# Reordering one step of a perceiver block kernel: row sums ahead of the second row maxima, PV ahead of the last quarter of a projection, tile 2's quantisation behind tile 0's third layer norm

## The chip, the cores and the metric

The kernel runs on one core of a Trainium2 chip. The metric is the time of one execution on the device in microseconds (us); the number given is the median of several executions. TensorE (PE) has a full clock of 2.4 GHz and a lower level of 1.2 GHz; the profile states the granted clock as a share of the full one.

## The reference

The input `x` is 16 x 64 rows of 1024 floats, the context 16 matrices of 1024 x 1024 floats (67 MB). Three residual blocks follow one another:

```python
# 1: cross attention stand-in: both sides fake-quantised to 8 bits
q1 = fake_quant(layernorm(x));  q2 = fake_quant(ctx_4096)
x = x + matmul(q1, q2)                       # per batch element
# 2: multi-query attention, 32 heads of 32, ALiBi, causal
qkv = layernorm(x) @ Wqkv
probs = softmax(where(causal, q @ k.T * scale + alibi, -1e30))
x = x + (probs @ v).reshape(B, S, H) @ Wo
# 3: routed one-bit feed-forward layer
h = layernorm(x);  r = softmax(h @ gate_w.T)
x = x + (h * (r @ in_scale)) @ sign(weight).T * (r @ out_scale) + bias
```

## The kernel before

The 1024 rows are cut into eight tiles of 128 rows (two batch elements, `b` = 0 and 1). Each tile needs 8 MB of context, which arrives as eight pieces of 1 MB in a ring of four slots: `load_context` on SyncE (SP) issues piece `c` of tile `t` to slot `c % 4`, after the piece that lay there has been rounded to 8 bits. That rounding is `conv(t, c)`, line 583 on ScalarE (ACT), now and then line 955 on VectorE (DVE). Two pieces make one call `context(t, pair)`, 8 matmuls at line 1407, and four calls are the product of block 1. I write "piece 2.4" for piece 4 of tile 2.

The quantised rows of a tile are made on DVE: `norm0_rows` (lines 979 and 983), then `norm0_quant` (lines 986 and 988), which writes `a16` and raises the semaphore `s_a`. From tile 2 on the rows are transposed by a DMA, `turn_over`, that SP issues when `s_a` has come. For tile 2 this call stands in SP's queue between the loads of pieces 2.0 to 2.3 (and the bias) and those of 2.4 to 2.7, so these four loads are issued only after it.

Every engine has its order of work written out by hand. The sequence is an entry, `step_0`, `step_1`, and then for tiles 2 to 7 an `opening` and a `burst` (tile 2 has no opening of its own). `step_1(s, ahead)` covers the heads of tile 1, the second half of tile 0's attention (`s`), all of tile 1's attention after the scores (`ahead`), both output projections, tile 0's feed-forward layer and the context product of tile 2. The names of its parts:

- `scores(s, h)` on PE, and on DVE `scores_in(t, h, b)` (line 1058) and `row_max(t, h, b)` (line 1063); `softmax_in(t, h)` is both for `b` = 0 and 1. `subtract_max` (line 334) runs on GpSimd (POOL) in this step, `exp` (line 605) on ACT, `row_sum` (lines 1068 and 1069) on DVE, `normalize` (line 485) on POOL. `pt` transposes the probabilities on PE (line 1426), `pt_hi` (line 567, ACT) and `pt_lo` (line 892, DVE) split them into two halves of 16 bits. `pv(s, h)` is the product with V (line 1507), `o_hi` (line 635, ACT) and `o_lo` (line 1081, DVE) split its result.
- `project(s, n, ks)`: half `n` of the output projection, three matmuls of 512 columns for each of the `ks` (lines 1371 to 1373); `low` is `k` = 0 to 3, `high` is 4 to 7. `x2(s, n)` on DVE adds it to `X` (line 1093) and takes half of the row statistics (line 959); after the second half POOL makes the inverse deviation, `inv_std(2, .)` (lines 458 and 459), and DVE `norm2` (line 971). `x1` (line 1007) and its statistics, `inv_std(1, .)` and `norm1` (line 971) are the same for block 1, and `t1` transposes what `norm1` wrote; `t1_hi` and `t1_lo` split that, and `kv(2)` begins the next tile.
- `t2` transposes what `norm2` wrote, `t2_copy` (line 567, ACT) takes it to `ln2T`, `router` (line 1554, PE), `router_max`, `router_exp` (line 697, ACT), `router_probs` (lines 1126 to 1132, DVE), `router_t` (line 1561), `rt_copy` (ACT), `inscale` (line 1573), `xs` (line 1140), `xs_hi` (ACT), `xs_lo` (DVE), `outscale` (line 1589), `outscale_copy` (line 613), `ffn` (line 1603), `result` (line 1154).

Matmul results lie in eight banks: `C` (two), `R` (four), and `T` (two, used in turn, so that each user waits until the one before it but one has been emptied). POOL's order at the end of the step is `with_bias(0)`, `with_row_sum(2)`, `inv_std(0, 3)`, `inv_std(2, 1)`, `inv_std(1, 2)`.

Of the kernel before, what the change touches and what calls it, by code (L numbers as in the profile page):

```python
# [139 lines left out]
def build(nc, x, context, wqkv, wo, w_t, bias, quant_in, small_in, scales_in, out):  # L140
    ctx = ExitStack()
    with ctx:
# [188 lines left out]
        def subtract_max(e, t, h, b):  # L331

            e.wait_ge(s_mx, piece(t, h, b) + 1)
            e.tensor_tensor(by_head(h, b), by_head(h, b), to_heads(h, b), ALU.subtract)\  # L334
                .then_inc(s_sub[b], 1)
# [100 lines left out]
        @block.gpsimd  # L436
        def _(e):

            chain = Chain(e, s_pool)
            link = chain.link  # L440

            e.memset(rs[:, 3:4], 0.0).then_inc(s_warm, 1)
            e.memset(bfill[:, BRING * H // 2:], BASE_PAIR).then_inc(s_fill, 1)
            for m in (ident, ident_h):
                link(e.memset(m[:, :], 0.0))
                link(e.affine_select(out=m[:, :], in_=m[:, :], compare_op=ALU.not_equal,
                                     fill=1.0, base=0, pattern=[[-1, P]], channel_multiplier=1))
            for hi, lo in vbd:
                link(e.memset(hi[:, :, :], 0.0))
                link(e.memset(lo[:, :, :], 0.0))  # L450
            for k, value in enumerate((-0.5, EPS)):
                link(e.memset(consts[:, k:k + 1], value))
            e.nop().then_inc(s_init, 1)

            def inv_std(k, t):

                e.wait_ge(s_st[k], t + 1)
                link(e.tensor_tensor(rstd[k][:, 0:1], mv[k][:, 1:2], consts[:, 1:2], ALU.add))  # L458
                e.tensor_tensor(rstd[k][:, 1:2], rstd[k][:, 0:1], consts[:, 0:1], ALU.pow)\
                    .then_inc(s_rstd[k], 1)  # L460

            def with_row_sum(t):

                e.wait_ge(s_row, t + 1)
                x_t = X[t % XBUFS]
                e.tensor_tensor(x_t[:, :], x_t[:, :], rowsum[:, 1:2].broadcast_to([P, H]), ALU.add)\  # L466
                    .then_inc(s_xc, 1)

            def with_bias(m):
                if m == 0:  # L470
                    e.wait_ge(s_bias, 16)
                e.wait_ge(s_xl2, m + 1 + (m == TILES - 1))
                x_m = X[m % XBUFS]
                e.tensor_tensor(x_m[:, :], x_m[:, :], bias_sb[:, :], ALU.add).then_inc(s_x2b, 1)

            def total(t, n):
                cols, x_t = slice(n * HALF, (n + 1) * HALF), X[t % XBUFS]
                e.wait_ge(s_fe, t * 2 + n + 1)
                if n == 0:
                    e.wait_ge(s_x2b, t + 1)  # L480
                e.tensor_tensor(x_t[:, cols], x_t[:, cols], XL[:, cols], ALU.add).then_inc(s_y, 1)  # L481

            def normalize(t, h, b):
                e.wait_ge(s_rcp, piece(t, h, b) + 1)
                e.tensor_tensor(by_head(h, b), by_head(h, b), to_heads(h, b), ALU.mult).then_inc(s_nrm, 1)  # L485

            def entry():
                inv_std(0, 0)
                with_row_sum(0)
                inv_std(0, 1)  # L490
                with_row_sum(1)

            def step_0(s):
                inv_std(1, 0)
                subtract_max(e, 0, 0, 0)
                subtract_max(e, 0, 0, 1)

            def step_1(s, ahead):
                subtract_max(e, 0, 1, 0)
                subtract_max(e, 0, 1, 1)  # L500
                normalize(0, 0, 0)
                normalize(0, 0, 1)
                inv_std(1, 1)
                normalize(0, 1, 0)
                normalize(0, 1, 1)
                inv_std(0, 2)
                subtract_max(e, 1, 0, 0)
                subtract_max(e, 1, 0, 1)
                subtract_max(e, 1, 1, 0)
                subtract_max(e, 1, 1, 1)  # L510
                normalize(1, 0, 0)
                normalize(1, 0, 1)
                normalize(1, 1, 0)
                normalize(1, 1, 1)
                inv_std(2, 0)
                with_bias(0)
                with_row_sum(2)
                inv_std(0, 3)
                inv_std(2, 1)
                inv_std(1, 2)  # L520
                total(0, 0)
                total(0, 1)

            def opening(s):
                m = s.i - 1
                subtract_max(e, m, 1, 1)
                normalize(m, 1, 0)
                normalize(m, 1, 1)
                with_bias(s.i - 2)
                total(s.i - 2, 0)  # L530
                inv_std(1, s.i)
                if s.next:
                    inv_std(0, s.i + 1)
                total(s.i - 2, 1)

            def burst(s):
                if not s.is_step(2):
                    inv_std(2, s.i - 1)
                if s.next:
                    with_row_sum(s.i + 1)  # L540
                subtract_max(e, s.i, 0, 1)
                normalize(s.i, 0, 0)
                normalize(s.i, 0, 1)

            def tail(s, last):
                t = TILES - 1
                subtract_max(e, t, 1, 1)
                normalize(t, 1, 0)
                normalize(t, 1, 1)
                with_bias(t - 1)  # L550
                total(t - 1, 0)
                inv_std(2, t)
                with_bias(t)
                total(t - 1, 1)
                x_t = X[t % XBUFS]
                for n in range(2):
                    cols = last_cols[n]
                    e.wait_ge(s_fe, t * 2 + n + 1)
                    e.tensor_tensor(x_t[:, cols], x_t[:, cols], XL[:, cols], ALU.add).then_inc(s_y, 1)

            run_steps(entry, step_0, step_1, opening, burst, tail)


        @block.scalar
        def _(e):
# [37 lines left out]
            def exp(t, h, b):  # L603
                e.wait_ge(s_sub[b], t * 2 + h + 1)
                e.activation(heads(h, b), heads(h, b), ACT.Exp).then_inc(s_exp, 1)  # L605
# [142 lines left out]
            def step_1(s, ahead):  # L748
# [27 lines left out]
                exp(1, 0, 1)  # L776
                sign(3)
                exp(1, 1, 0)
                exp(1, 1, 1)
                pt_hi(ahead, 0, 0)  # L780
                pt_hi(ahead, 0, 1)
                conv(2, 0)
                o_hi(ahead, 0)
                pt_hi(ahead, 1, 0)
# [2 lines left out]
                conv(2, 2)  # L787
                o_hi(ahead, 1)
                conv(2, 3)
                conv(2, 4)  # L790
                t2_copy(s, 0)
                t2_copy(s, 1)
                router_exp(s)
                conv(2, 5)
                rt_copy(s)
# [89 lines left out]
        def _(e):  # L885
# [325 lines left out]
            def step_1(s, ahead):  # L1211
# [23 lines left out]
                softmax_in(1, 0)  # L1235
                o_lo(s, 1)
                q_lo(s, 1)
                softmax_in(1, 1)
                row_sum(1, 0, 0)
                row_sum(1, 0, 1)  # L1240
                norm0_rows(2)
                row_sum(1, 1, 0)
                row_sum(1, 1, 1)
                pt_lo(ahead, 0, 0)
                pt_lo(ahead, 0, 1)
                norm0_quant(2)
                o_lo(ahead, 0)
                x2(s, 0)
                x2(s, 1)
                pt_lo(ahead, 1, 0)  # L1250
                pt_lo(ahead, 1, 1)
                norm2(s)
                o_lo(ahead, 1)
                stats0(3)
                router_max(s)
# [3 lines left out]
                xs(s, 1)  # L1259
                xs_lo(s, 0)  # L1260
                xs_lo(s, 1)
                x2(ahead, 1)
                x1(ahead)
                norm1(ahead)
                result(ahead, 0)
                t1_lo(ahead, 0)
# [82 lines left out]
        def _(e):  # L1349
# [5 lines left out]
            low, high = range(KT // 2), range(KT // 2, KT)  # L1355
# [304 lines left out]
            def step_1(s, ahead):  # L1660
# [13 lines left out]
                tk(s)  # L1674
                query(s, 0, high[:2])
                pt(s, 1, 0)
                pt(s, 1, 1)
                query(s, 0, high[2:])
                query(s, 1, low)
                pv(s, 1)  # L1680
                scores(s, 0)
                query(s, 1, high)
                project(s, 0, low)
                scores(s, 1)
                project(s, 1, low)
                project(s, 0, high)
                pt(ahead, 0, 0)
                pt(ahead, 0, 1)
                project(s, 1, high)
                pv(ahead, 0)  # L1690
                pt(ahead, 1, 0)
                pt(ahead, 1, 1)
                project(ahead, 0, low)
                pv(ahead, 1)
                project(ahead, 1, low)
                t2(s)
                context(2, 0)
                router(s)
                project(ahead, 0, high)
                router_t(s)  # L1700
                context(2, 1)
                inscale(s, 0)
                inscale(s, 1)
                project(ahead, 1, high)
                context(2, 2)
                context(2, 3)
                ffn(ahead, 0, low)
                outscale(ahead, 0)
                outscale(ahead, 1)
                ffn(ahead, 0, high)  # L1710
                ffn(ahead, 1, low)
                t1(ahead)
                ffn(ahead, 1, high)
# [125 lines left out]
```

## Time and profile before

| | before |
|---|---|
| median of 3 runs | 408.12 us (407.4 to 408.24) |
| profiled execution, own time | 407.38 us |
| its span | 405.6 us |
| PE matmul busy | 362.7 us, 89% of the span |
| DVE / ACT / POOL busy | 312.1 / 253.8 / 133.5 us |
| transfers | 91.56 MB, 226 GB/s over the span |

The span is divided into busy time of each engine; an engine's work is strictly in the order of its own queue, and between engines semaphores decide. `step_1` runs from about 55 us to 134 us, where `kv(2)` begins. The tables below name for each instruction its start, its duration and, in brackets, how long its engine had been idle and what ended that.

### The profile page before, as it was taken

To read this page: it belongs to the slowest core of one execution; us is meant where nothing else is said; L and a number is where in the kernel's file an instruction comes from. 1 tells how busy PE (TensorE), PEld (TensorE's weight loads), DVE (VectorE), ACT (ScalarE), POOL (GpSimd) and SP (SyncE) were. 2 spreads that over 40 slices of the span, in tenths; PEclk is the share of its full clock that TensorE was granted. 3 is DMA by queue.
4 is the path that set the end of the run, shared out by engine and by line. 5 is a ranking of instruction groups with operands and counts; after the bars stand their busy time and mean duration, and the time that the engine had idled before them with its cause. 6 is when DMAs were issued, how large, how long until landed. Compare 5 with 4: busy or idle time off the path is not lost.

```text
span 405.6 us, 10034 instructions
## 1 busy us (share of the span) xinstructions
PE 362.7 (89%) x4162; PEld 233.9 (58%) x4162; DVE 312.1 (77%) x592; ACT 253.8 (63%) x306; POOL 133.5 (33%) x148
## 2 busy tenths in 40 slices
PE   0438977999789999999999999999999999999996
PEld 0113943874444874578557855696559655974444
DVE  6888798999846788679876997589858975496353
ACT  3857985867787877783887388648865741334021
POOL 5320043426321226312541246124612371026041
PEclk9957999999999999999999999999999999999999
DMA  7999999399999499857867587748665000100002
GB/s 303 410 373 408 409 405 391 114 322 412 311 367 347 190 288 404 302 178 196 298 229 240 147 269 263 228 153 294 225 244 131 10 2 6 50 2 0 2 1 105
DMA packets 30243, 91.56 MB, mean 226 GB/s; under 512 B 8112, under 2 KB 8496, under 8 KB 30192
## 3 DMA queue, kind: packets, MB, share of 16 engines
q1 hardware_dynamic: 28320, 84.42, 58.5%
q10 hardware_dynamic: 1872, 6.40, 4.2%
q8 instruction: 39, 0.64, 0.6%
q14 instruction: 12, 0.10, 0.1%
HBM read 85.05 MB, written 4.19 MB: 220 GB/s over the span
## 4 chain that ended last, share of the span: by engine, by line
PE 60%; DVE 15%; DMA 9%; ACT 7%; SPq 4%; issue 3%; POOL 0%; DVEq 0%; ACTq 0%; POOLq 0%
DMA ring<-ctx 9%; PE R L1603 9%; PE T L1426 6%; PE R L1371 5%; PE R L1372 5%; PE R L1373 5%; PE C L1407 4%; ACT b L583 4%; PE R L1462 4%; PE R L1465 3%; PE R L1464 3%; PE T L1507 3%; SPq L371 2%; PE R L1491 2%; PE R L1378 1%
## 5 line engine op out<-in xcount | busy, mean ns | idle before, releaser
L583 ACT ACTIVATE b<-ring,quant,qpar 128x2048 uint8<-128x2048 f32 x61 | 126.4, 2093 | 14.3 <-DMA ring<-ctx 8.2
L1462 PE MATMUL R<-T_hi,Wqkv_hi 128*128 128x128 f16 x448 | 77.9, 220 | 0.0
L1465 PE MATMUL R<-T_hi,Wqkv_lo 128*128 128x128 f16 x448 | 77.7, 219 | 0.0
L1464 PE MATMUL R<-T_lo,Wqkv_hi 128*128 128x128 f16 x448 | 77.7, 219 | 0.0
L1407 PE MATMUL C<-b,aT 128*64 128x512 f16 x256 | 35.7, 411 | 12.9 <-ACT b L583 6.3
L485 POOL TENSOR_TENSOR Pr<-Pr,mx 128x512 f32<-128x512 f32 x32 | 35.4, 1118 | 30.5 <-DVE mx L1069 30.5
L334 POOL TENSOR_TENSOR Pr<-Pr,mx 128x512 f32<-128x512 f32 x20 | 20.7, 1044 | 74.7 <-DVE mx L1063 74.7
L1462 PEld LDWEIGHTS R<-T_hi,Wqkv_hi 128*128 128x128 f16 x448 | 43.9, 98 | 2.0
L1464 PEld LDWEIGHTS R<-T_lo,Wqkv_hi 128*128 128x128 f16 x448 | 43.9, 98 | 0.2
L1465 PEld LDWEIGHTS R<-T_hi,Wqkv_lo 128*128 128x128 f16 x448 | 43.8, 98 | 0.0
L1371 PE MATMUL R<-Wo,attT_hi 128*128 128x512 f16 x112 | 42.5, 379 | 0.6 <-DVE attT_lo L1081 0.5
L1372 PE MATMUL R<-Wo,attT_hi 128*128 128x512 f16 x112 | 42.4, 379 | 0.0
L1373 PE MATMUL R<-Wo,attT_lo 128*128 128x512 f16 x112 | 42.4, 379 | 0.0
L1603 PE MATMUL R<-sgn,XS_hi 128*128 128x512 fp8e4 x96 | 36.6, 381 | 0.0
L1603 PE MATMUL R<-sgn,XS_lo 128*128 128x512 fp8e4 x96 | 36.4, 379 | 0.0
L959 DVE BATCH_NORM_STATS2 st<-X 128x6 f32<-128x512 f32 x48 | 33.1, 689 | 1.4
L481 POOL TENSOR_TENSOR X<-X,XL 128x512 f32<-128x512 f32 x14 | 17.8, 1271 | 41.0 <-DVE XL L1154 40.1
L458 POOL TENSOR_TENSOR small<-small,consts 128x1 f32<-128x1 f32 x24 | 4.6, 192 | 77.1 <-DVE small L966 77.1
L1407 PEld LDWEIGHTS C<-b,aT 128*64 128x64 f16 x256 | 13.5, 115 | 27.1 <-ACT b L583 8.3
L466 POOL TENSOR_TENSOR X<-X,small 128x1024 f32<-128x1024 f32 x8 | 16.6, 2075 | 34.2 <-DVE small L991 34.2
L567 ACT ACTIVATE PT_hi<-T 128x512 f16<-128x512 f32 x32 | 17.6, 593 | 15.9 <-PE T L1426 15.8
L605 ACT ACTIVATE Pr<-Pr 128x512 f32<-128x512 f32 x32 | 19.8, 625 | 11.3 <-DVE Pr L334 10.5
(172 smaller groups left out, 845.4 us busy)
## 6 DMA issues: line engine op xcount, KB each, us to landing
ring<-ctx SPq DMA_DIRECT2D x64, 1024.0 KB, 7.7
ring<-L_attn_Wo SPq DMA_DIRECT2D x4, 1024.0 KB, 9.3
ring<-L_ffn_weight SPq DMA_DIRECT2D x4, 1024.0 KB, 5.2
Wo<-L_attn_Wqkv SPq DMA_DIRECT2D x7, 544.0 KB, 15.2
X<-x ACTq DMA_DIRECT2D x6, 512.0 KB, 4.6
out<-X ACTq DMA_DIRECT2D x6, 512.0 KB, 6.2
X<-x SPq DMA_DIRECT2D x2, 512.0 KB, 11.5
sgn<-L_attn_Wqkv SPq DMA_DIRECT2D x1, 544.0 KB, 18.0
```

The lines of the kernel that those rows point to most:

```text
L485: e.tensor_tensor(by_head(h, b), by_head(h, b), to_heads(h, b), ALU.mult).then_inc(s_nrm, 1)
L583: e.activation(b8[:, c % BRING, :], ring[:, slot, :], ACT.Identity, scale=qR2, bias=qZ2).then_inc(s_rf[slot], 1)
L959: link(e.bn_stats(st[k][:, h, :], src[:, h * HALF:(h + 1) * HALF]))
L1371: e.matmul(dst, lhs[0], rhs[0], start=first, stop=False)
L1372: e.matmul(dst, lhs[0], rhs[1], start=False, stop=False)
L1373: return e.matmul(dst, lhs[1], rhs[0], start=False, stop=last)
L1407: ins = e.matmul(C[b * S:(b + 1) * S, n, :], lhs(b), b16[:, (2 * pair + b) % BRING, k, n * HALF:(n + 1) * HALF], start=first, stop=last)
L1426: last = e.transpose(T[:, bank, n * P:(n + 1) * P], src, ident[:, :])
L1462: e.matmul(dst, hi, rows[0], start=k == 0 and g == 0, stop=False, skip_group_check=True)
L1464: e.matmul(dst, hi, rows[1], start=False, stop=False, skip_group_check=True)
L1465: last = e.matmul(dst, lo, rows[0], start=False, stop=k == KT - 1, skip_group_check=True)
L1603: last = e.matmul(ffn_to(s.i - 2, n), XS[part][:, k, :], sgn[:, k, n * HALF:(n + 1) * HALF], start=k == 0 and part == 0, stop=k == KT - 1 ...
```

## The change

Orders alone change, in `step_1`; no instruction is added or removed. POOL: the normalisation of the first half of tile 1's heads goes ahead of the subtraction of the maxima of the second half. ACT: `exp(1, 1, 1)` goes behind the two `pt_hi` of the first half; `conv(2, 4)` goes behind the two `t2_copy`. DVE: the row sums of the first half go ahead of the row maxima of the second half, the last row sum goes behind two `pt_lo`, `norm0_quant(2)` goes from ahead of `o_lo(ahead, 0)` to behind `norm2(s)`, and `x1(ahead)` goes ahead of `x2(ahead, 1)`. PE: as listed. SP's queue is left as it is.

```diff
 POOL    inv_std(0, 2)
         subtract_max(e, 1, 0, 0)
         subtract_max(e, 1, 0, 1)
+        normalize(1, 0, 0)
+        normalize(1, 0, 1)
         subtract_max(e, 1, 1, 0)
         subtract_max(e, 1, 1, 1)
-        normalize(1, 0, 0)
-        normalize(1, 0, 1)
 ACT     exp(1, 1, 0)
-        exp(1, 1, 1)
         pt_hi(ahead, 0, 0)
         pt_hi(ahead, 0, 1)
+        exp(1, 1, 1)
         conv(2, 0)
...
-        conv(2, 4)
         t2_copy(s, 0)
         t2_copy(s, 1)
+        conv(2, 4)
         router_exp(s)
 DVE     q_lo(s, 1)
-        softmax_in(1, 1)
+        scores_in(1, 1, 0)
+        scores_in(1, 1, 1)
         row_sum(1, 0, 0)
         row_sum(1, 0, 1)
+        row_max(1, 1, 0)
+        row_max(1, 1, 1)
         norm0_rows(2)
         row_sum(1, 1, 0)
-        row_sum(1, 1, 1)
         pt_lo(ahead, 0, 0)
         pt_lo(ahead, 0, 1)
-        norm0_quant(2)
+        row_sum(1, 1, 1)
         o_lo(ahead, 0)
         x2(s, 0)
         x2(s, 1)
         pt_lo(ahead, 1, 0)
         pt_lo(ahead, 1, 1)
         norm2(s)
+        norm0_quant(2)
         o_lo(ahead, 1)
...
         xs_lo(s, 1)
+        x1(ahead)
         x2(ahead, 1)
-        x1(ahead)
         norm1(ahead)
 PE      pt(s, 1, 0)
+        query(s, 0, high[2:3])
         pt(s, 1, 1)
-        query(s, 0, high[2:])
+        query(s, 0, high[3:])
         query(s, 1, low)
         pv(s, 1)
+        query(s, 1, high[:1])
         scores(s, 0)
-        query(s, 1, high)
+        query(s, 1, high[1:])
...
-        project(s, 1, high)
+        project(s, 1, high[:3])
         pv(ahead, 0)
+        project(s, 1, high[3:])
         pt(ahead, 1, 0)
         pt(ahead, 1, 1)
         project(ahead, 0, low)
         pv(ahead, 1)
         project(ahead, 1, low)
         t2(s)
+        project(ahead, 0, high)
+        router(s)
         context(2, 0)
-        router(s)
-        project(ahead, 0, high)
+        context(2, 1)
         router_t(s)
-        context(2, 1)
         inscale(s, 0)
         inscale(s, 1)
         project(ahead, 1, high)
         context(2, 2)
         context(2, 3)
         ffn(ahead, 0, low)
+        ffn(ahead, 0, high)
         outscale(ahead, 0)
         outscale(ahead, 1)
-        ffn(ahead, 0, high)
         ffn(ahead, 1, low)
         t1(ahead)
```

## Rows read from the trace of the kernel before

**Rows 1.** Busy time by stretch, with count; last columns: granted clock, DMA share, GB/s
```profile
84.00:111.60 27.60, 24.10 (x208) 13.64 (x209) 24.90 (x43) 19.92 (x19) 11.52 (x11) 1.00 0.98 359
111.60:134.00 22.40, 20.68 (x188) 9.84 (x187) 13.10 (x27) 18.36 (x17) 5.48 (x9) 1.00 0.97 355
134.00:180.00 46.00, 45.23 (x571) 30.97 (x568) 35.60 (x74) 35.13 (x47) 16.46 (x17) 1.00 0.80 276
180.00:222.00 42.00, 41.93 (x511) 28.11 (x508) 34.17 (x69) 29.09 (x37) 15.19 (x16) 1.00 0.71 233
```

**Rows 2.** Timeline of PE: start, duration, instruction, idle time before it
```profile
104.39 0.63 PE L1426 MATMUL T<-ident,Pr 128*128 128x128 f32 x4 [1.69 <-DVE attT_lo L1081]
114.70 0.81 PE L1554 MATMUL T<-ln2T,small_sb 128*8 128x32 f32 x64 [1.04 <-ACT ln2T L567]
122.53 1.92 PE L1407 MATMUL C<-b,aT 128*64 128x512 f16 x16
131.06 1.09 PE L1426 MATMUL T<-ident,tok 128*128 128x128 f32 x8 [0.69 <-DVE tok L971]
```

**Rows 3.** Timeline of DVE from tile 1's split probabilities to tile 0's norm 2
```profile
100.25 1.24 DVE L892 TENSOR_TENSOR PT_lo<-T,PT_hi 128x512 f16<-128x512 f32 x2
101.41 0.55 DVE L986 TENSOR_SCALAR a<-a 128x1024 int16<-128x1024 int16 x1
101.98 1.28 DVE L988 TENSOR_SCALAR_CACHE_REDUCE a<-a,qpar 128x1024 f16<-128x1024 int16 x1
103.50 0.75 DVE L1081 SCALAR_TENSOR_TENSOR attT_lo<-T,attT_hi 128x256 f16<-128x256 f32 x2
108.45 0.81 DVE L971 TENSOR_SCALAR XL<-X,small 128x1024 f32<-128x1024 f32 x1
```

**Rows 4.** Timeline of SP's queue around the transposing transfer of tile 2
```profile
103.30 1.33 SPq L385 DMA_TRANSPOSE aT<-a  x1
104.69 0.57 SPq L371 DMA_DIRECT2D ring<-ctx  x1
```

**Rows 5.** Issues in 104.6 to 105 us: KB, us to landing (piece 2.4)
```profile
ring<-ctx SPq DMA_DIRECT2D x1, 1024.0 KB, 5.2
aT<-a SPq DMA_TRANSPOSE x1, 3.4
```

**Rows 6.** Busy time by stretch, columns as in group 1
```profile
116.00:120.00 4.00, 4.00 (x29) 1.80 (x27) 2.52 (x9) 3.88 (x4) 0.00 (x0) 1.00 1.04 416
```

**Rows 7.** Timeline of ACT from piece 2.3 to the feed-forward input
```profile
110.00 4.07 ACT L583 ACTIVATE b<-ring,quant,qpar 128x2048 uint8<-128x2048 f32 x2
113.98 1.06 ACT L567 ACTIVATE ln2T<-T 128x512 f32<-128x512 f32 x2
116.05 0.30 ACT L697 ACTIVATE rt<-rl,small 128x8 f32<-128x8 f32 x1 [1.01 <-DVE small L1120]
118.58 4.07 ACT L583 ACTIVATE b<-ring,quant,qpar 128x2048 uint8<-128x2048 f32 x2
122.55 1.13 ACT L567 ACTIVATE XS_hi<-ln2T 128x512 f16<-128x512 f32 x2
```

**Rows 8.** Timeline of DVE, from the split input to tile 2's norm 1
```profile
117.26 0.17 DVE L1132 TENSOR_TENSOR rstack<-rt,rstack 128x16 f16<-128x16 f32 x1
123.19 1.29 DVE L892 TENSOR_TENSOR XS_lo<-ln2T,XS_hi 128x512 f16<-128x512 f32 x2 [2.11 <-ACT XS_hi L567]
124.41 0.68 DVE L1093 SCALAR_TENSOR_TENSOR X<-R,X 128x512 f32<-128x512 f32 x1
126.09 1.27 DVE L1007 SCALAR_TENSOR_TENSOR X<-C,qpar,X 128x1024 f32<-128x1024 f32 x1
130.19 0.81 DVE L971 TENSOR_SCALAR tok<-X,small 128x1024 f32<-128x1024 f32 x1 [1.01 <-POOL small L459]
```

**Rows 9.** Timeline of POOL, the two inverse deviations at the step's end
```profile
126.25 0.19 POOL L458 TENSOR_TENSOR small<-small,consts 128x1 f32<-128x1 f32 x1 [11.85 <-DVE small L966]
129.26 0.19 POOL L458 TENSOR_TENSOR small<-small,consts 128x1 f32<-128x1 f32 x1 [2.18 <-DVE small L966]
```

**Rows 10.** The longest idle time of PE at full clock: timeline, then the stretch
```profile
24.45 1.92 PE L1407 MATMUL C<-b,aT 128*64 128x512 f16 x8 [5.06 <-ACT b L583]
...
22.00:24.00 2.00, 0.00 (x0) 0.00 (x0) 1.86 (x5) 1.69 (x1) 0.16 (x1) 0.57 0.97 307
```

## The prediction

> **What bounds the kernel now.** I read the busy time by stretch first. From 180 us on PE is busy 41.93 of 42.00 us, and in 134 to 180 us 45.23 of 46.00 [rows 1]: from tile 2 on the kernel is a full PE queue, and what `step_1` gains or loses arrives at the end nearly whole. At most 0.8 us could be made good in tile 2's burst, where PE still waits a little. From 84 to 134 us PE is busy 24.10 and 20.68 of 50.0 us [rows 1], so 5.2 us idle: that is the most this change can win. In the same stretches the transfers are at a share of 0.98 and 0.97 [rows 1], which no later stretch shows. The reader should see both: PE has holes here, and the DMA has none to spare.
>
> Then the timelines. PE's holes of interest are 1.69 us ahead of `pt(ahead, 1, 1)`, which waits for `o_lo(ahead, 0)`; 1.04 us ahead of `router`, which waits for `ln2T`; and the one ahead of `t1(ahead)` at 131.06 us, which waits for `norm1` [rows 2]. Between them `context(2, 2)` and `context(2, 3)` run without a gap, 122.53 to 124.45 [rows 2]. Yet they are just in time: ACT rounds 2.6 and 2.7 in one row 118.58 to 122.65 [rows 7], and the second call starts at about 123.4, only 0.8 us later. Last, SP's queue: the transposing transfer goes out at 103.30, the moment `norm0_quant(2)` ends (101.98 + 1.28 = 103.26), and the load of 2.4 at 104.69, right behind it [rows 3, 4].
>
> **Part 1, the front of the step (all moves up to `pv(ahead, 1)`): a gain on PE.** Row sums ahead of row maxima: on DVE two maxima of 0.6 us come out of the way, so the first `normalize` starts some 1.2 us sooner and the hole between the two first `pt` closes. The three quarters of `project` go under `pt_hi` and `pt_lo`, the query slices fill two short waits; the waits they fill end on DVE, so they save 0.4 us at the second `scores`. The large piece is `norm0_quant(2)` out of the way of `o_lo`: 0.55 + 1.28 + 0.28 us, about 2.1 [rows 3]. The price on this side is that `exp(1, 1, .)` comes about 2 us later, because POOL normalises first; `row_sum(1, 1, 1)` then stands behind `pt_lo` and costs it nothing. Followed instruction by instruction: `pt_lo` ends at 100.4 (1.0 sooner than 101.41, [rows 3]), `row_sum(1, 1, 1)` to 101.2, `o_lo` 101.5 to 102.2, and `pt(ahead, 1, 1)` starts at 102.35 where it was 104.39 [rows 2]. PE is **2.0 us ahead** here, and stays so through `project(ahead, 1, low)`.
>
> **Part 2, router behind the projection: another 1.0 us, on paper.** `t2_copy` no longer waits for `conv(2, 4)` (2.04 us of the pair 110.00 to 114.07, [rows 7]) and `project(ahead, 0, high)`, 12 matmuls, covers it: the hole of 1.04 [rows 2] goes. Up to there PE is about 3 us ahead of before.
>
> **Part 3, `norm0_quant(2)` behind `norm2(s)`: what SP makes of it.** Between the old place of `norm0_quant` and its new one stand `o_lo`, two `x2`, two `pt_lo` and `norm2`, which took DVE from 103.50 to 109.26 without a hole, 5.8 us [rows 3]. The new start is `row_sum(1, 1, 1)`'s end 101.2, 0.3 for `o_hi`, and 5.8: 107.3. It takes 1.9 (101.41 to 103.26), so `s_a` comes at **109.3 instead of 103.3, 6.0 us later**. Nothing on DVE suffers, and `aT` itself is not missed: 109.3 plus 3.4 to 4.7 us for the transfer [rows 4, 5] is 112.7 to 114.0, and `context(2, 0)` now comes at 114.2, behind `router`. But SP is a queue, and behind `turn_over(2)` stand the loads of 2.4 to 2.7. Piece 2.4 went out at 104.69 and landed 5.2 us later, 109.9 [rows 4, 5]. Now it goes out 1.4 us after `s_a`, at 110.7, and lands at **115.9**. The DMA, at 0.98 before, stands nearly empty from the landing of the bias (about 106) to 111.
>
> The other three slots are free by then (conv of 2.1 to 2.3 ends by 110.3), so 2.5 to 2.7 go out at once behind 2.4 and follow at the full rate. 1.05 MB at 416 GB/s [rows 6] is 2.53 us each: 2.7 lands at 115.9 + 7.6 = 123.5. Before, its rounding began at about 120.6, half way in the pair of [rows 7]. So `conv(2, 7)` starts **3.0 us later** and ends at 125.6. The bounds: if the loads were to land at once after 2.4, ACT alone would need 115.9 + 3 x 2.04 + 0.6 (`router_exp`, `rt_copy`) = 122.6, still 2.0 later than before; if they came at 355 GB/s, the mean of these stretches [rows 1], 2.7 lands at 124.8, 4.2 later. I take 3.0, since a full queue is what the row with 416 shows.
>
> Two more things hang on this. `router_exp` now stands behind `conv(2, 4)` on ACT, which ends at 117.95, so it comes 1.9 us later than 116.05 [rows 7], and `router_t`, 1.2 us behind it (117.43 + 0.7 there [rows 7, 8]), at 119.4. PE has finished `context(2, 1)` at about 116.2 and idles 3.2 us, then again until `rt_copy`, which stands behind `conv(2, 5)`, 120.8. All that PE gained is given back here; it reaches `context(2, 2)` at 124.0 and waits for 2.7 until 125.6.
>
> Behind `conv(2, 7)` ACT makes `xs_hi`, then DVE `xs_lo`: from 122.65 to 124.41 before [rows 7, 8], 1.8 us. New: 127.4, which is 3.0 later. `context(2, 3)` is done by then (126.6).
>
> **Part 4, `x1(ahead)` ahead of `x2(ahead, 1)`: the queue of POOL.** `t1(ahead)` needs `norm1`, that needs `inv_std(1, 2)`, and on POOL `inv_std(2, 1)` still stands in front of it and needs the statistics of `x2(ahead, 1)`. Before, from 124.41 to `t1` at 131.06: `x2(ahead, 1)` 1.68, `x1` with statistics and hop 3.17 (126.09 to 129.26), `inv_std` 0.93 to 130.19, `norm1` 0.87, in sum 6.65 [rows 2, 8, 9]; `inv_std(2, 1)` ran at 126.25 beside the work [rows 9]. Now: `x1` 3.10, `x2(ahead, 1)` 1.84 with the hop to POOL, `inv_std(2, 1)` 0.87, then `inv_std(1, 2)` 0.93, `norm1` 0.87: 7.6. So **0.95 us more** than with the old order. The move could only pay where `x1` can start before `x2(ahead, 1)` could, and both are ready when `xs_lo` ends. `outscale` waits for `x2(ahead, 1)`'s first instruction at about 131.3 and `ffn(ahead, 1, low)` ends at 133.5, still ahead of `t1`, so moving it behind `ffn(ahead, 0, high)` hides that. The sum is thus bounded: 0.95 if both are ready, 0 if `x1` could start 1 us sooner than now, which `xs_lo` excludes.
>
> **The sum.** `t1` at 127.4 + 7.6 = 135.0 instead of 131.06: 3.0 + 0.95 = **4.0 us later**, and `kv(2)`, 2.7 us behind it in both, at 137.8 instead of 133.8. The profiled execution, 407.38 us (span 405.6), becomes 411.4. It lay 0.7 us under the median of the runs, so the median becomes **412.1**.
>
> **The rivals.** *The clock falls.* PE would be idle 3.2 us and, but for one transpose, 4.6 us, 116.2 to 120.8. The one idle time that long at full clock in this trace, 5.06 us before 24.45, had the granted clock at 0.57 of full in 22 to 24 us, so it went to the 1.2 GHz level under 3 us after PE stopped [rows 10]. Against it: mine is shorter and has work in it. If it falls, `inscale` and `project(ahead, 1, high)` (3.1 us) take 6.2 and end at 127 instead of 124, both context calls follow, and `x1` starts at 128.7 instead of 127.4: 1.3 us more, **413.4**. The Trainium skill (TensorE: Matmul & The Clock Gate, HAM oscillation) warns that PE-idle gaps between bursts drop the array to its slow level; by that rule this rival would be the likelier one, and the row agrees for a gap of 5.06 us, while none here shows 3.2.
>
> *The loads catch up.* ACT's own queue is the bound, 2.0 instead of 3.0, and tile 2's burst gives 0.4 back: **410.7**.
>
> *Faster.* If pieces 2.4 to 2.7 were not what is late, PE's lead decides: about 3 us up to `router`, less 0.95 for part 4, so 2.1 gained: **406.0**. It decides once 2.7 is rounded by the time PE reaches `context(2, 3)`, about 120.5; for that `s_a` would have to come by about 104.5. Only a `norm0_quant` that DVE reaches 5 us sooner than the rows add up to would do it. For it speaks that a DMA wait is often hidden; against it that this one has 0.8 us of cover.
>
> *Nothing in sum.* Lead and loss cancel to within 0.8 us: **408.1**. That needs 2.7 to land at about 120.
>
> **How the numbers follow.** Forecast 412.1 with a chance of 0.50; the clock 0.25; catching up 0.12; faster 0.08; nothing 0.05. The range takes in the first three and their bounds: below, 2.0 + 0.95 less 0.8 is 410.3; above, 4.2 + 0.95 is 413.3, and 413.4 with the clock, with another 0.8 for a clock that falls sooner: 414.2. About 0.2% (0.8 us) is what a measurement of this kernel can tell from no change. Faster 0.08, same 0.05, slower 0.87.
>
> **What would show it.** Right: the transposing transfer issued near 109.3; DMA nearly idle 106 to 111; piece 2.4 rounded from about 116; a PE hole ahead of `router_t` of about 3 us; `pt(ahead, 1, 1)` near 102.4; two `inv_std` back to back before `norm1`; `kv(2)` near 137.8. Wrong: the transfer before 107, or ACT rounding 2.4 to 2.7 with no wait for the ring, or `x1` starting well ahead of the end of `xs_lo`. A fallen clock around 120 us would show the first rival.

## The result and the profile after

| | before | changed |
|---|---|---|
| median of 4 runs each | 407.90 us (407.4 to 408.24) | 413.84 us (413.54 to 414.49) |
| profiled execution, own time | 407.38 us | 413.63 us |
| its span | 405.6 us | 411.8 us |
| PE matmul busy | 362.7 us | 366.3 us |
| DVE / ACT / POOL busy | 312.1 / 253.8 / 133.5 us | 311.2 / 253.6 / 134.7 us |

The ratio is 1.0147, with a 95% interval of 1.0132 to 1.0162: the changed kernel is **5.9 us slower**. The forecast was 412.1 in a range of 410.3 to 414.2.

Where the time went is seen in the same order as before. First SP's queue, the transposing transfer and what follows it (start, duration), then its landings (KB, us from issue), which answer to [rows 4, 5]:

```profile
96.11 0.47 SPq L414 DMA_DIRECT2D bias_sb<-L_ffn_bias  x1
109.51 1.34 SPq L385 DMA_TRANSPOSE aT<-a  x1
110.89 26.55 SPq L371 DMA_DIRECT2D ring<-ctx  x10
```

```profile
ring<-ctx SPq DMA_DIRECT2D x1, 1024.0 KB, 5.4
aT<-a SPq DMA_TRANSPOSE x1, 3.1
```

The transfer goes out at 109.51 instead of 103.30, and with it the load of 2.4 at 110.89 instead of 104.69. From about 106 us, when the bias has landed, the DMA stands still. This is the busy time by stretch (columns as in [rows 1]):

```profile
84.00:111.60 27.60, 25.38 (x217) 14.52 (x214) 24.93 (x44) 20.71 (x21) 13.44 (x12) 1.00 0.77 292
...
104.00:106.00 2.00, 2.00 (x11) 0.78 (x8) 1.79 (x5) 2.00 (x2) 0.00 (x0) 1.00 0.21 78
106.00:108.00 2.00, 1.52 (x15) 0.74 (x15) 2.00 (x4) 2.00 (x2) 0.77 (x3) 1.00 0.00 0
108.00:110.00 2.00, 2.00 (x11) 0.88 (x10) 1.93 (x5) 2.00 (x3) 2.00 (x1) 1.00 0.00 0
```

PE did win in front: it is busy 25.38 us up to 111.6, where it was 24.10 [rows 1]. But the DMA share fell from 0.98 to 0.77. ACT then waits for the ring at every one of the four pieces (in brackets: idle time, and what ended it), where [rows 7] show no such wait:

```profile
116.29 2.10 ACT L583 ACTIVATE b<-ring,quant,qpar 128x2048 uint8<-128x2048 f32 x1 [4.36 <-DMA ring<-ctx]
118.29 0.28 ACT L697 ACTIVATE rt<-rl,small 128x8 f32<-128x8 f32 x1
119.36 2.10 ACT L583 ACTIVATE b<-ring,quant,qpar 128x2048 uint8<-128x2048 f32 x1 [0.79 <-DMA ring<-ctx]
121.37 0.25 ACT L567 ACTIVATE rT<-T 32x128 f16<-32x128 f16 x1
122.88 2.10 ACT L583 ACTIVATE b<-ring,quant,qpar 128x2048 uint8<-128x2048 f32 x1 [1.27 <-DMA ring<-ctx]
125.44 2.10 ACT L583 ACTIVATE b<-ring,quant,qpar 128x2048 uint8<-128x2048 f32 x1 [0.46 <-DMA ring<-ctx]
```

The timeline of PE shows what is made of that, and answers to [rows 2]: one hole is smaller (0.94 for 1.69), the one ahead of `router` is gone, and two new ones stand ahead of `router_t` and `inscale`:

```profile
102.96 0.63 PE L1429 MATMUL T<-ident,Pr 128*128 128x128 f32 x4 [0.94 <-DVE attT_lo L1081]
...
119.79 0.22 PE L1564 MATMUL T<-ident_h,rstack 128*32 128x128 f16 x1 [3.41 <-DVE rstack L1132]
121.72 1.01 PE L1576 MATMUL T<-rT,scales 32*128 32x128 f16 x8 [1.71 <-ACT rT L567]
...
137.24 1.09 PE L1429 MATMUL T<-ident,tok 128*128 128x128 f32 x8 [1.40 <-DVE tok L971]
```

In the second of these holes the granted clock falls to its 1.2 GHz level, at about 121.1 us, and stays there for about 6.8 us (`inscale` takes 1.01 us where the same eight take 0.60 at full clock, in e1 below). Busy time by stretch:

```profile
118.00:120.00 2.00, 0.21 (x1) 0.09 (x1) 1.26 (x6) 1.21 (x3) 0.00 (x0) 1.00 1.03 410
120.00:122.00 2.00, 0.29 (x5) 0.32 (x5) 0.94 (x2) 1.61 (x2) 0.00 (x0) 0.77 1.01 406
122.00:124.00 2.00, 2.00 (x11) 0.97 (x10) 1.29 (x2) 1.12 (x1) 0.00 (x0) 0.50 1.04 414
124.00:126.00 2.00, 2.00 (x6) 0.65 (x5) 0.00 (x0) 1.54 (x2) 0.00 (x0) 0.50 1.02 406
126.00:128.00 2.00, 2.00 (x7) 0.56 (x7) 0.00 (x0) 2.00 (x3) 0.00 (x0) 0.52 1.03 414
```

Last, DVE from `x1` to `norm1`, and POOL's two inverse deviations, which answer to [rows 8, 9]. `x1` waits 0.47 us for `context(2, 3)`, which is late because the projection ahead of it ran at the lower clock; then both inverse deviations run one behind the other, after `x2(ahead, 1)`:

```profile
129.85 1.28 DVE L1007 SCALAR_TENSOR_TENSOR X<-C,qpar,X 128x1024 f32<-128x1024 f32 x1 [0.47 <-PE C L1410]
...
136.37 0.81 DVE L971 TENSOR_SCALAR tok<-X,small 128x1024 f32<-128x1024 f32 x1 [1.79 <-POOL small L459]
```

```profile
134.66 0.19 POOL L458 TENSOR_TENSOR small<-small,consts 128x1 f32<-128x1 f32 x1 [21.63 <-DVE small L966]
134.92 0.55 POOL L459 TENSOR_TENSOR small<-small,consts 128x1 f32<-128x1 f32 x1
135.44 0.19 POOL L458 TENSOR_TENSOR small<-small,consts 128x1 f32<-128x1 f32 x1
135.71 0.55 POOL L459 TENSOR_TENSOR small<-small,consts 128x1 f32<-128x1 f32 x1
```

`t1` is 137.24 - 131.06 = 6.2 us late, and so is the end: the span grew by 6.2. After tile 2's `kv` nothing is won or lost: in 186 to 228 us PE is busy 41.93 of 42.00 us, as in [rows 1].

### The profile page after: what moved, and what is told of

The parts are those of the page before. It is cut to its first block, busy times and chain, and to the rows that moved or that the text cites. A ratio compares the mean times of both kernels' runs of the same rounds, so it can differ in the third digit from the quotient of the medians.

```text
span 411.8 us, 10034 instructions
## 1 busy us (share of the span) xinstructions
PE 366.3 (89%) x4162; PEld 236.1 (57%) x4162; DVE 311.2 (76%) x592; ACT 253.6 (62%) x306; POOL 134.7 (33%) x148
## 4 chain that ended last, share of the span: by engine, by line
PE 63%; DVE 18%; DMA 7%; ACT 5%; issue 4%; POOL 2%; SPq 1%; DVEq 0%; POOLq 0%; ACTq 0%
PE R L1606 9%; DMA ring<-ctx 7%; PE T L1429 6%; PE R L1374 6%; PE R L1375 5%; PE R L1376 5%; PE C L1410 5%; PE R L1465 5%; PE R L1468 4%; PE R L1467 4%; PE T L1510 3%; PE R L1494 2%; DVE st L959 2%; ACT b L583 2%; PE R L1381 2%
## 5 line engine op out<-in xcount | busy, mean ns | idle before, releaser
L485 POOL TENSOR_TENSOR Pr<-Pr,mx 128x512 f32<-128x512 f32 x32 | 36.0, 1133 | 31.1 <-DVE mx L1069 31.1
L334 POOL TENSOR_TENSOR Pr<-Pr,mx 128x512 f32<-128x512 f32 x20 | 21.6, 1088 | 72.0 <-DVE mx L1063 72.0
L1374 PE MATMUL R<-Wo,attT_hi 128*128 128x512 f16 x112 | 43.5, 388 | 0.6 <-DVE attT_lo L1081 0.5
L1375 PE MATMUL R<-Wo,attT_hi 128*128 128x512 f16 x112 | 43.5, 388 | 0.0
L1376 PE MATMUL R<-Wo,attT_lo 128*128 128x512 f16 x112 | 43.5, 388 | 0.0
```

Source lines behind the costliest of these rows:

```text
L1374: e.matmul(dst, lhs[0], rhs[0], start=first, stop=False)
L1375: e.matmul(dst, lhs[0], rhs[1], start=False, stop=False)
L1376: return e.matmul(dst, lhs[1], rhs[0], start=False, stop=last)
```

## The experiments

Each ratio is to runs of the kernel before on the same chip, taken in turn with it. Where two versions are compared below, it is by these ratios unless the text says otherwise. Theory A is that of the prediction: the late `s_a` holds SP's queue, and POOL's order holds norm 1.

**e1: the quantisation back, the rest of the change kept.**

```diff
 DVE     row_sum(1, 1, 1)
+        norm0_quant(2)
         o_lo(ahead, 0)
...
         norm2(s)
-        norm0_quant(2)
```

> The changed kernel, with norm0_quant(2) alone put back ahead of o_lo(ahead, 0). Theory A (the late s_a holds SP's queue, and with it the loads of pieces 2.4 to 2.7): s_a at about 103, piece 2.4 issued at about 104.5, piece 2.7 rounded from about 120 instead of 125.4; no transfer wait on ACT over 1 us; no fallen clock at 120 us; 408 us, some 5.8 less than the changed kernel, and within 0.5 of the kernel before, since what PE wins in front is lost to x1 standing ahead of x2(ahead, 1). Theory B (the loss is made by the other moves, the order of x1 and x2 and of router and context above all, and the loads are late only in step with it): at least 412 us.

Measured: 407.78 us against 408.15 before, ratio 0.9992 (0.9975 to 1.0008). This one call is worth the whole loss, some 6 us, and all the other moves together make no difference that this measurement shows. The timelines of e1, of SP and of ACT, show the transfer issued 1 us sooner than in [rows 4], and pieces 2.6 and 2.7 rounded in one go with no wait for the ring, 0.8 us sooner than in [rows 7]:

```profile
102.34 1.33 SPq L385 DMA_TRANSPOSE aT<-a  x1
```

```profile
117.82 4.07 ACT L583 ACTIVATE b<-ring,quant,qpar 128x2048 uint8<-128x2048 f32 x2
```

**e2: SP's queue reordered, `s_a` as late as in the changed kernel.**

```diff
 SP      e.dma_start(bias_sb, ...)
-        turn_over(2)
-        load_context(2, 4, ITEMS - 4)
+        load_context(2, 4, 3)
+        turn_over(2)
+        load_context(2, 7, 1)
```

> The changed kernel, with SP's queue alone reordered: turn_over(2) between the loads of 2.6 and 2.7 instead of ahead of 2.4. s_a stays at 109.5. Theory A: piece 2.4 issued at about 101.5 when its slot is free, 2.4 to 2.6 landed by 114, 2.7 rounded from about 119.5 to 121.5, x1 from about 123.5, norm 1 to t1 7.4 us behind it, so t1 at about 131: 407.5 to 408, equal to the kernel before, although s_a is 6 us late. Theory B (s_a late is dear in itself, through aT and context(2, 0)): at least 411 us.

Measured: 408.05 us, ratio 1.0016 (0.9994 to 1.0038). The quantisation ends as late as in the changed kernel (the transfer is issued at 109.32), yet the loss is gone: it is not the late `s_a` that costs, it is what stands behind it in the queue. The timeline of SP in e2 shows three loads ahead of the transfer, and that of PE a wait of 1.59 us for `aT`. It costs little: `x1` starts at 124.00, where it was 123.64 in e1:

```profile
101.38 7.02 SPq L371 DMA_DIRECT2D ring<-ctx  x3
109.32 1.41 SPq L385 DMA_TRANSPOSE aT<-a  x1
```

```profile
115.88 1.92 PE L1411 MATMUL C<-b,aT 128*64 128x512 f16 x16 [1.59 <-DMA aT<-a]
```

**e4: the quantisation alone, on the kernel before.**

```diff
 DVE     pt_lo(ahead, 0, 1)
-        norm0_quant(2)
         o_lo(ahead, 0)
...
         norm2(s)
+        norm0_quant(2)
```

> The kernel before, with norm0_quant(2) alone moved behind norm2(s). Theory A: s_a at about 107.5 to 109.5, loads of 2.4 to 2.7 late as in the changed kernel, router late too since t2_copy stands behind conv(2, 4): 413 us or more, 5 above the kernel before, and the granted clock falls to half near 118 us. Theory B (the other moves make the loss): under 409.5 us.

Measured: 416.02 us, ratio 1.0185 (1.0157 to 1.0214), 7.5 us above before and worse than the whole change. Without the new order of `router` and `t2_copy`, `ln2T` stands behind `conv(2, 4)` and PE has one hole of 5.44 us ahead of `router`. So the change's other moves do soften the blow, by 1.6 us by the two ratios, even with the loss that `x1` brings. The timeline of PE in e4:

```profile
120.22 1.04 PE L1554 MATMUL T<-ln2T,small_sb 128*8 128x32 f32 x64 [5.44 <-ACT ln2T L567]
```

**e3, e9 and e11: the order of `x1` and `x2`.** e3 puts `x2(ahead, 1)` back ahead of `x1(ahead)` in the changed kernel; e9 makes the exchange alone in the kernel before; e11 leaves DVE as changed and exchanges the two inverse deviations on POOL:

```diff
 POOL    inv_std(0, 3)
+        inv_std(1, 2)
         inv_std(2, 1)
-        inv_std(1, 2)
```

> The changed kernel, with x2(ahead, 1) again ahead of x1(ahead). Theory A: inv_std(2, 1) runs beside x1 again, which gives 0.75 us, and x2 fills the 0.5 us in which x1 waited for the slow context call: 412.6 us, 1.2 less than the changed kernel. Rival (norm 1 is covered by ffn on PE, the order does not matter): 413.8, as the changed kernel.

> The kernel before, with x1(ahead) alone moved ahead of x2(ahead, 1). Theory A (inv_std(1, 2) stands behind inv_std(2, 1) on POOL, which waits for x2's statistics): xs_lo and context(2, 3) end together at about 124.4, then 7.4 us to t1 instead of 6.65; outscale waits for x2 until 127.5, and in the old order of PE ffn(ahead, 0, high) stands behind it, so PE has 3.5 us of work left at 128 and t1 comes at about 131.9: 408.9 to 409.2, 0.75 to 1.0 above before. Rival (x1 sooner is norm 1 sooner, as the order says): 406.5, 1.6 less than before.

> The changed kernel, with POOL's inv_std(1, 2) ahead of inv_std(2, 1) and nothing else. Theory A: norm 1 follows x2(ahead, 1) at once, at 134.6 instead of 136.4, and t1 comes when PE has done outscale and ffn(ahead, 1, low), at 135.9 instead of 137.2: 412.5 us, 1.3 less than the changed kernel. Rival (POOL's order is not on the path): 413.8.

Measured: e3 412.54 us, ratio 1.0113 (1.0091 to 1.0135), so 1.4 less than the changed kernel. e9 409.32 us against 407.75 before, ratio 1.0039 (1.0024 to 1.0054), 1.6 slower. e11 412.31 us, ratio 1.0103 (1.0088 to 1.0119), 1.8 less than the changed kernel. The rivals of all three fall. e3 and e11 come out as theory A has it: in the changed kernel the move was a loss because POOL's order was not changed with it.

e9 does not show that. In its profile norm 1 does wait 1.79 us for POOL, but it is done at 131.9, and PE reaches `t1` at 133.84 without waiting for it. What holds PE up is the hole where the exchange puts it, ahead of `outscale`, which waits for `x2`, and the clock that falls behind that hole. The timelines of PE and DVE in e9:

```profile
128.38 0.37 PE L1589 MATMUL R<-scales,rT 32*128 32x512 f16 x1 [1.72 <-DVE X L1093]
133.84 1.04 PE L1426 MATMUL T<-ident,tok 128*128 128x128 f32 x8
```

```profile
131.11 0.81 DVE L971 TENSOR_SCALAR tok<-X,small 128x1024 f32<-128x1024 f32 x1 [1.79 <-POOL small L459]
```

Its ten runs lie in two groups. The four with a mean granted clock of 1.00 took 408.35 to 408.46 us; the six with 0.979 to 0.996 took 409.21 to 410.56. So at full clock the exchange costs some 0.7 us, and the rest of the 1.6 goes with a fallen clock. The mean does not say where the clock fell: it falls in the kernel's entry too, and runs of the kernel before with a mean of 1.00 were up to 0.5 us faster than the others. At full clock PE would be at `t1` at about 132.1 (an estimate: 16 matmuls of 0.216 us from 128.69), within 0.2 us of norm 1, so e9 cannot tell POOL's order from `outscale`'s wait even there.

**e5, e12 and e13: the price of the clock.** e5 and e13 are one kernel, the changed one with work of no use in the new holes; e12 is the changed kernel again, beside e13.

```diff
 PE      context(2, 1)
+        e.wait_ge(s_stt, piece(1, 1, 1) + 1)
+        keep_clock(14)
         router_t(s)
+        keep_clock(6)
         inscale(s, 0)
```

> The changed kernel, with matmuls that compute nothing of use in PE's idle time: 14 of 512 columns ahead of router_t (3.0 us) and 6 ahead of inscale (1.3 us), into a bank that is free, so that the granted clock stays at full between 120 and 128 us. Theory A (the late piece 2.7 decides, and the slow clock costs only what x1 waits for context(2, 3), 0.47 us): 413.4 us, 0.45 less than the changed kernel. Theory C (the fallen clock is the 1.9 us by which the changed kernel lies above the forecast): 412.2 us or less.

> The changed kernel once more, beside the next run, for the price of the clock. Theory A (the fallen clock costs what x1 waits for context(2, 3), 0.5 to 1.0 us by two profiles) and theory C (it costs the 1.7 us that lay between the medians of two separate calls) both expect 413.8 here; they part in the next run.

> The changed kernel with 14 and 6 idle-time matmuls ahead of router_t and inscale, as before, now on the same chip and in the same rounds as the changed kernel. Theory A: 0.5 to 1.0 us below it. Theory C: 1.4 us or more below it.

Measured: e5 412.13 us, ratio 1.0108 (1.0092 to 1.0123); e12 413.82, ratio 1.0147 (1.0120 to 1.0174); e13 412.46, ratio 1.0103 (1.0083 to 1.0124). The clock stayed at full in both filled kernels from 112 to 132 us. The medians put its price at 1.7 us where the two kernels ran on different occasions, and at 1.4 side by side. The profiles show it where `x1` waits for `context(2, 3)`. From the start of `conv(2, 7)` to that of `x1` it took 3.87 and 3.85 us with the filling, 4.41, 4.73 and 4.84 in three profiles without it (the changed kernel, e12, e11): 0.6 to 1.0 us. In e14 below, the changed kernel with one more wait in SP's queue, it took 5.46: there the clock was low for 10.2 us (118.1 to 128.3) instead of 6.8, and the price is 1.6. These are the two instructions in the timelines of ACT and DVE, first of e13, then of e12:

```profile
124.97 2.10 ACT L583 ACTIVATE b<-ring,quant,qpar 128x2048 uint8<-128x2048 f32 x1 [0.46 <-DMA ring<-ctx]
128.82 1.28 DVE L1007 SCALAR_TENSOR_TENSOR X<-C,qpar,X 128x1024 f32<-128x1024 f32 x1
```

```profile
124.48 2.10 ACT L583 ACTIVATE b<-ring,quant,qpar 128x2048 uint8<-128x2048 f32 x1 [0.46 <-DMA ring<-ctx]
129.21 1.28 DVE L1007 SCALAR_TENSOR_TENSOR X<-C,qpar,X 128x1024 f32<-128x1024 f32 x1 [0.78 <-PE C L1410]
```

So the number in theory A's first expectation (0.45) was too small, and theory C's bounds are met in e5 and, by the medians (1.36 for 1.4), just missed in e13, but its claim that the clock is the whole 1.9 us is not shown. The intervals of the ratios are 0.6 to 1.1 us to either side; whether the 0.4 to 1.1 us between profile and medians belongs to the clock of this stretch stays open (the entry's clock, as seen in e9, can move a run by up to 0.5).

**e14: the load of 3.0 held back.**

```diff
 SP      load_context(2, 4, ITEMS - 4)
+        e.wait_ge(s_ld[3], (uses(2, 7) + 1) * 16)
```

> The changed kernel, with one wait more in SP's queue: the load of piece 3.0 is issued only when piece 2.7 has landed. Theory D (2.5 to 2.7 landed 9.15 us after 2.4 and not 7.6 because the loads of 3.0 and 3.1, issued from 118.4 on, share the DMA with them): they land in 7.6 to 8.0 us after 2.4, x1 starts 1.2 to 1.5 us sooner, and since tile 3's pieces have cover the time falls by 0.7 to 1.2 us, to about 412.8. Rival (a piece takes that long by itself, behind others): the distance stays at 8.9 to 9.2 us and the time at 413.8 or more.

Measured: 414.51 us, ratio 1.0148 (1.0117 to 1.0178), and 124.96 - 116.03 = 8.93 us from the rounding of 2.4 to that of 2.7: theory D falls. No later load was in flight, and still 2.7 came no sooner. The stretches show where the time is: the bulk had come by about 123, and the landing waited some 1.9 us for a small remainder. Busy time by stretch of e14, columns as before:

```profile
120.00:122.00 2.00, 0.00 (x0) 0.00 (x0) 0.69 (x1) 1.96 (x1) 0.00 (x0) 0.50 1.02 410
122.00:124.00 2.00, 1.61 (x10) 1.05 (x11) 0.92 (x2) 1.84 (x3) 0.00 (x0) 0.50 0.51 203
124.00:125.00 1.00, 1.00 (x3) 0.30 (x2) 0.37 (x1) 0.58 (x2) 0.00 (x0) 0.50 0.03 12
```

**e10 and e15: two versions from these findings.** e10 is e1 with the exchange on POOL, e15 is e2 with it.

> The changed kernel with norm0_quant(2) back ahead of o_lo(ahead, 0), as in the first experiment, and on POOL inv_std(1, 2) ahead of inv_std(2, 1). Theory A: inverse deviation 1 runs beside x2(ahead, 1), norm 1 is ready at 129.1 and PE reaches t1 at 129.5 without waiting, where it waited 1.4 us in the first experiment: 406.3 us, 1.5 less than the first experiment and 1.8 less than before. Rival (PE, or the outscale that waits for x2, is the bound): 407.8, as the first experiment.

> The changed kernel with both cures that leave norm0_quant(2) where the change put it: SP's turn_over(2) between the loads of 2.6 and 2.7, and POOL's inv_std(1, 2) ahead of inv_std(2, 1). If the two losses are separate and add, the second run's 408.05 less the 1.4 that the exchange on POOL gave twice: 406.7 us. If PE's wait for aT (1.59 us in the second run) is the bound there, 408.

Measured: e10 406.45 us against 407.75 before, ratio 0.9965 (0.9951 to 0.9978); e15 406.51 against 408.11, ratio 0.9966 (0.9950 to 0.9982). Both beat both kernels, by 1.3 to 1.6 us against before and some 7 against the changed one. In the timelines of e10, of DVE and of PE, norm 1 comes at 128.55 without a wait, and `t1` has none either:

```profile
128.55 0.80 DVE L971 TENSOR_SCALAR tok<-X,small 128x1024 f32<-128x1024 f32 x1
```

```profile
129.74 1.04 PE L1429 MATMUL T<-ident,tok 128*128 128x128 f32 x8
```

## Why the prediction was right, point by point

| term | forecast | measured |
|---|---|---|
| `pt(ahead, 1, 1)` | 102.35 | 102.96 |
| transposing transfer issued | 109.3 | 109.51 |
| 2.4 lands, rounding begins | 115.9 | 116.29 |
| from there to the rounding of 2.7 | 7.6 | 9.15 |
| from there to the end of `xs_lo` | 3.9 | 3.9 |
| `x1` waits for `context(2, 3)` | 0 | 0.5 |
| from `x1` to `t1` | 7.6 | 7.39 |
| `t1` | 135.0 | 137.24 |
| median | 412.1 | 413.84 |

- **Part 1 and 2, PE's lead:** right. The order of all calls up to `router` gained nearly what it was said to gain; of the 0.6 us by which `pt(ahead, 1, 1)` is later than forecast some 0.4 are differences between executions: the first `scores` of the step starts at 84.99 here and at 84.54 before, and between 83.77 and 84.99 in the other profiles, whatever their order. Counted from those `scores`, the gain is 1.9 us for the 2.0 forecast. e1 shows what the lead is worth when the loads are in time: with `t1` at 131.03 it ends in the wait for norm 1.
- **Part 3, SP's queue:** right. e1 and e4 show that this one call makes the loss, and e2 that it does so through the loads behind it in SP's queue and not through `aT`. **Its size was off by one term:** 7.6 us for pieces 2.5 to 2.7 at 416 GB/s. They took 8.8 to 9.2 us in all seven profiles of this order. The step that failed was to take the rate of the DMA for the distance between landings: the rate was 410 GB/s in these 9.1 us, and the pieces still landed further apart. The bound of 355 GB/s (8.9 us) would have met the number, by luck, since the rate was not what was low. Two slips changed nothing: 107.3 + 1.9 is 109.2 and not 109.3, and the 4.7 us for a transfer is not in the rows named, it is that of tile 3. The rivals for the cause of the distance: sharing with later loads is excluded by e14; that a piece is complete only when the slowest of the DMA engines has done its part would fit its stretches, but no run separated the engines, and the cause stays open.
- **Part 4, POOL's queue:** right in the mechanism and near in size: 7.39 for 7.6 us in the profile, and 1.4 and 1.8 us by e3 and e11 for a forecast of 0.95. What the sum left out is that `x2` in front also fills time in which `x1` has to wait (0.47 us in the profile). e9's 1.6 us is no measure of it, as said there.
- **The rival "the clock falls"** happened, in the holes and with the length given for them (3.41 us and one transpose, then 1.71, where 3.2 and 1.4 were said). It had a chance of 0.25 against 0.50 for the case without it, and that was the wrong way round: the clock fell in these holes in all five profiles of this order that left them unfilled (the changed kernel, e3, e11, e12, e14). The row with 5.06 us could not have given the chance. It was one execution, and in the same hole of the entry, 4.5 to 5.3 us long, the clock fell in eight of the fourteen profiles, 2.9 to 3.6 us after PE stopped, and not in the other six (e2, e3, e5, e10, e11, e12). The Trainium skill (TensorE: Matmul & The Clock Gate, HAM oscillation) warns of such gaps; the five profiles agree, the six do not. Forecast without clock 412.1, with it 413.4; measured 413.84. The rival's path was not quite the measured one: it had `x1` wait 1.3 us, and in the profile it waited 0.47, since PE would have waited for the rounding of 2.7, which ended at 127.54, at full clock too.
- **The sum:** in the profile `t1` came 2.24 us after the forecast of 135.0. Of these, 0.4 are the first landing, 1.55 the distance to the last, 0.5 the wait that the clock made, less 0.2 behind `x1`.
- **"The loads catch up":** no; they came later than forecast.
- **"Faster" and "nothing in sum":** excluded for this kernel by the result. But e10 and e15 show the condition under which the first was right: with `s_a` in time (or out of the loads' way) and POOL's order matched, the rest of the change gains 1.3 to 1.6 us on the kernel before.
- **The end moves with `kv(2)`:** right. The 0.8 us that tile 2's burst might have given back were not given back: 6.2 us at `t1`, 6.2 us in the span.

## What to carry to other kernels

A step that moves behind others takes with it everything that waits for its result, and on a DMA queue that is also whatever stands behind the transfer: follow the semaphore into SP's queue before trusting a gain on DVE. When two items change places on one engine, look for the engine that serves both in a fixed order and change it too. Where a forecast opens a hole on PE, price the fallen clock as well, and do not take its chance from one hole of one trace: the same hole saw it fall in one execution and not in the next. And where several loads queue together, do not divide their bytes by the rate to know when the last has landed.

## What the runs showed of the hardware

- The granted clock can fall after a hole of 1.72 us. In e9 PE stopped at 126.66, and the clock was at half from about 128.8 to 132.2, by the busy time by stretch below. It does not always: a hole of 1.69 us in the same profile (102.78 to 104.47) and one of 1.80 in e1 (101.64 to 103.44) saw no fall.

```profile
126.00:128.00 2.00, 0.67 (x3) 0.09 (x1) 1.82 (x4) 0.72 (x1) 0.00 (x0) 1.00 1.03 395
128.00:130.00 2.00, 1.61 (x5) 0.66 (x6) 1.14 (x3) 1.21 (x2) 0.52 (x2) 0.71 0.99 369
130.00:132.00 2.00, 2.00 (x7) 0.63 (x5) 0.81 (x1) 1.80 (x1) 0.92 (x3) 0.50 0.61 240
```

- A hole of 4.5 to 5.3 us, the same in every kernel here, saw the clock fall in eight of fourteen profiles and not in six. In e5 PE stopped at 19.61 and ran again at 24.08, and the clock was at 1.00 in every stretch from 20 to 60 us.
- Four loads of 1 MB were issued in the changed kernel within 2 us, behind the transposing transfer, onto a DMA that had been idle. The first landed 5.4 us after its issue, and the others 3.07, 3.52 and 2.56 us apart (by the starts of the roundings that waited for them). From the first landing on the rate was 406 to 414 GB/s, which by itself would be 2.5 us each.
- The DMA made good nothing of the late issue, though free slots let the other three loads follow at once. Piece 2.4 was issued 6.2 us later than before, and 2.7 landed 6.1 us later: at 125.4, where before it was issued at 112.11 and took 7.2 us (its landing, below), so 119.3. Its rounding came only 4.8 us later because before the piece had lain 1.3 us until ACT was free:

```profile
ring<-ctx SPq DMA_DIRECT2D x1, 1024.0 KB, 7.2
```
